# New places for the side pieces of an audio-tower kernel, and its softmax sums sent through 100 partitions for the reciprocal

## The reference, cut to what matters

```python
x.shape == (8, 120000)                       # 8 batches, 1500 frames of 80 samples
h = gelu(layernorm(frames @ W.T + b) * gamma + beta)          # tokenizer, 1500 x 256
n = layernorm(h)
Q, K, V = n @ Wq.T + bq, n @ Wk.T + bk, n @ Wv.T + bv         # 16 heads of 16
attn = softmax(Q K^T / 4)                                     # 1500 x 1500 per head
h = h + (attn @ V) @ Wo.T + bo
out = layernorm(h + ffn(layernorm(h)))
```

## Time and profile before

| | us |
|---|---|
| median of 3 runs | 2575.2 (2572.72 to 2577.77) |
| the profiled execution | 2566.03 |
| its span, first to last instruction | 2564.3 |
| PE busy | 2270.0 (89%) |
| ACT busy | 2154.9 (84%) |
| DVE busy | 1222.3 (48%) |
| POOL busy | 374.1 (15%) |
| DMA queues of SP, share of 16 engines | 19.1% |

### The profile page before, as it was taken

How to read it: one execution, slowest core, us unless ns; L and a number is a source line. 1 busy time by engine, 2 the same in 40 slices (tenths; PEclk the granted TensorE clock), 3 DMA queues, 4 the chain that set the end, 5 groups by cost and what they waited for, 6 DMA issues and landing times.

```text
span 2564.3 us, 48095 instructions
## 1 busy us (share of the span) xinstructions
PE 2270.0 (89%) x19500; PEld 680.2 (27%) x19500; DVE 1222.3 (48%) x2362; ACT 2154.9 (84%) x2332; POOL 374.1 (15%) x495
## 2 busy tenths in 40 slices
PE   4589998999989998899988999899998999898892
PEld 1222222222322222222222222222222222222221
DVE  6444435544465444643456444654446444452224
ACT  0099997999969998899978999699997999799991
POOL 2211002211121111210122110211112111120002
PEclk7799999999989999999989999899998999999997
DMA  2402211222122122122112221212212212111101
GB/s 60 128 17 63 63 37 39 53 63 63 38 69 56 42 59 53 46 77 53 41 45 53 63 63 39 58 40 56 67 33 70 54 51 53 52 47 31 31 5 30
DMA packets 89956, 132.09 MB, mean 52 GB/s; under 512 B 12295, under 2 KB 69702, under 8 KB 89726
## 3 DMA queue, kind: packets, MB, share of 16 engines
q1 hardware_dynamic: 87190, 127.11, 19.1%
...
## 4 chain that ended last, share of the span: by engine, by line
PE 40%; issue 34%; ACT 9%; POOL 9%; DVE 4%; POOLq 1%; DMA 1%; SPq 1%; DVEq 0%; ACTq 0%
PE PS L834 19%; PE PS L810 12%; PE PS L771 5%; ACT prob L476 4%; ACT prob L473 3%; POOL sq L367 3%; POOL Y L375 2%; PE PS L780 2%; POOL rs L377 2%; DVE HL L553 1%; POOL rs L348 1%; DVE HL L551 1%; POOLq L376 1%; DMA qk_halves_scratch<-HL 1%; ACT prob L481 1%
## 5 line engine op out<-in xcount | busy, mean ns | idle before, releaser
L834 PE MATMUL PS<-prob,Vst 125*32 125x500 f32 x9216 | 1149.8, 602 | 1.9 <-ACT prob L476 1.1
L481 ACT ACTIVATE prob<-PS 125x1000 f32<-125x1000 f32 x768 | 775.0, 1009 | 208.9 <-PE PS L810 208.3
L810 PE MATMUL PS<-QA,KA 64*125 64x500 f16 x4608 | 783.1, 413 | 105.2 <-DMA KA<-qk_halves_scratch 46.0
L473 ACT ACTIVATE prob<-PS 125x1000 f32<-125x1000 f32 x768 | 773.6, 1007 | 108.3 <-PE PS L810 108.2
L476 ACT ACTIVATE prob<-PS 125x1000 f32<-125x1000 f32 x768 | 782.8, 1019 | 0.0
L810 PEld LDWEIGHTS PS<-QA,KA 64*125 64x125 f16 x4608 | 258.7, 133 | 896.1 <-ACT prob L473 419.2
L603 DVE RECIPROCAL On<-Den 128x125 f32<-128x125 f32 x384 | 344.5, 918 | 10.2 <-issue 2.7
L834 PEld LDWEIGHTS PS<-prob,Vst 125*32 125x32 f32 x9216 | 221.9, 109 | 441.4 <-issue 272.9
L551 DVE TENSOR_SCALAR HL<-PS,b_qk 128x500 f16<-128x500 f32 x96 | 70.9, 738 | 397.9 <-PE PS L771 333.8
L367 POOL TENSOR_TENSOR sq<-HL 128x2000 bf16<-128x2000 f16 x24 | 84.5, 3522 | 1184.8 <-DVE HL L553 1184.8
L771 PE MATMUL PS<-zT,w_qk 128*32 128x500 f32 x1536 | 196.4, 593 | 1.2 <-DVE zT L542 1.2
...
## 6 DMA issues: line engine op xcount, KB each, us to landing
qk_halves_scratch<-HL SPq DMA_DIRECT2D x384, 125.0 KB
QA<-qk_halves_scratch SPq DMA_DIRECT2D x64, 375.0 KB, 5.0
KA<-qk_halves_scratch SPq DMA_DIRECT2D x64, 375.0 KB, 7.2
oT<-On SPq DMA_DIRECT2D x384, 31.2 KB, 2.0
...
```

The lines of the kernel that those rows point to most:

```text
L473: act.activation(prob[0:T, 6 * p:6 * p + 2, :], PS[0:T, 0:2, 0:QC], ACT.Exp, scale=scl)\
L481: act.activation(prob[0:T, 6 * p + 4:6 * p + 6, :], PS[0:T, 4:6, 0:QC], ACT.Exp, scale=scl)\
L810: last = pe.matmul(PS[0:T, bank, 0:QC], KA[rows, G % 2, h // 2, t * T:(t + 1) * T], QA[rows, G % 2, h // 2, c * QC:(c + 1) * QC], start=Tr ...
L834: last = pe.matmul(PS[lo:lo + 2 * HD, 6 + n % 2, 0:QC], Vst[:, b % 2, t, g * HG + j, :], prob[0:T, (HG * t + j) % 12, :], start=(t == 0), ...
```

## The change

Four things change together.

1. The plan. Places of nearly all pieces move, NORMS and GELU too. `tok` 0 and 1 of a batch now run in units 10 and 11 of the batch two before.
2. Reciprocals. `take_sums` no longer shuffles; it only copies. SP sends the 4 rows of sums (4 x 500 values) from `Osb` to a tile `thin` of 100 partitions by 20 values at the head of the unit after (`spread_sums`), DVE takes the reciprocal of `thin` in round 3 (`invert`), SP sends it back to rows 0, 32, 64 and 96 of `Den` in round 3 (`gather_sums`), and in round 5 DVE shuffles each of these rows over its 32 partitions and multiplies with `Osb` (`normalise`).
3. SP's order. `store_attended` moves to round 5, all `load_group` to the end of the list of the second unit of the group before (unit 10 for the next batch's first group), `store_out` of the third chunk to unit 3.
4. `tok_norm` subtracts the mean (and frees the bank) before it waits for POOL's root.

```diff
-    for j, r in enumerate((0, 2, 3, 4)):
+    for j, r in enumerate((0, 2, 4, 6)):
         place(11, r, "out", j)
         place(0, r, "out", 4 + j)
-    for j in range(2):
-        place(11, 5 + j, "tok", j)
-        place(0, 5 + j, "tok", 2 + j)
-        place(1, 2 * j, "tok", 4 + j)
-    place(1, 4, "out", 8)
+    place(10, 4, "tok", 0)
+    place(11, 3, "tok", 1)
+    place(0, 3, "tok", 2)
     for j in range(3):
-        place(1, 6, "out", 9 + j)
-    place(2, 4, "turn", 0)
-    place(2, 6, "turn", 1)
-    place_qk(0, 3, 0, 2)
-    place_qk(1, 3, 3, 4)
+        place(1, 2 * j, "tok", 3 + j)
+        place(2, 1, "out", 9 + j)
+    place(1, 6, "out", 8)
+    place(2, 6, "turn", 0)
+    place(3, 0, "turn", 1)
+    place_qk(0, 3, 2, 3)
+    place_qk(1, 3, 4, 5)
     place(3, 6, "val", 0)
     place_qk(2, 4, 0, 2)
     place_qk(3, 4, 3, 4)
-    place(4, 6, "val", 1)
-    place(5, 0, "val", 2)
+    place(4, 5, "val", 1)
+    place(4, 6, "val", 2)
+    place(5, 0, "val", 3)
     place(5, 1, "norm", 0)
-    place(5, 2, "val", 3)
-    place(5, 3, "turn", 2)
-    place(5, 4, "turn", 3)
-    place(5, 6, "val", 4)
-    place_qk(4, 6, 0, 2)
-    place_qk(5, 6, 3, 4)
+    place(5, 2, "turn", 2)
+    place(5, 3, "turn", 3)
+    place_qk(4, 5, 4, 6)
+    place_qk(5, 6, 0, 2)
+    place_qk(6, 6, 3, 4)
+    place(6, 5, "val", 4)
     place(6, 6, "val", 5)
-    place_qk(6, 7, 0, 2)
-    place_qk(7, 7, 3, 4)
-    place(7, 6, "val", 6)
-    place(8, 0, "val", 7)
+    place_qk(7, 7, 0, 2)
+    place(7, 3, "val", 6)
+    place(7, 4, "val", 7)
+    place(7, 6, "turn", 4)
+    place(8, 0, "turn", 5)
     place(8, 1, "norm", 1)
-    place(8, 2, "turn", 4)
-    place(8, 3, "turn", 5)
-    place_qk(8, 8, 4, 6)
-    place_qk(9, 9, 0, 2)
-    place_qk(10, 9, 3, 4)
-    place(9, 6, "val", 8)
-    place_qk(11, 10, 0, 2)
-    place(10, 3, "val", 9)
-    place(10, 4, "val", 10)
-    place(10, 6, "val", 11)
-    place(11, 1, "norm", 2)
-    place(11, 5, "flag", 0)
-    NORMS = {(2, 0): 0, (4, 6): 1, (7, 6): 2}
-    GELU = (1, 7)
+    place_qk(8, 8, 2, 3)
+    place_qk(9, 8, 4, 5)
+    place(8, 6, "val", 8)
+    place_qk(10, 9, 0, 2)
+    place_qk(11, 9, 3, 4)
+    place(9, 6, "val", 9)
+    place(10, 0, "val", 10)
+    place(10, 1, "norm", 2)
+    place(10, 2, "val", 11)
+    place(10, 6, "flag", 0)
+    NORMS = {(2, 3): 0, (4, 4): 1, (6, 6): 2}
+    GELU = (2, 2)
...
+            def spread_sums(n):
+                sp.wait_ge(s_ov, at(s_ov, n + 1))
+                sp.dma_start(thin[:, :], Osb[HD:128:2 * HD, :].rearrange("j (s c) -> j s c", s=25)).then_inc(s_pk, 16)
+
+            def gather_sums(n):
+                sp.wait_ge(s_rc, at(s_rc, n + 1))
+                sp.dma_start(Den[0:128:2 * HD, :].rearrange("j (s c) -> j s c", s=25), thin[:, :]).then_inc(s_up, 16)
...
-                    if u % NC == 1 and u < NU - 2:
-                        load_group(b * NG + u // NC + 1)
-                    if u < 3 and b > 0:
-                        store_out(b - 1, u)
+                    if n > 0:
+                        spread_sums(n - 1)
+                    if u in (0, 1, 3) and b > 0:
+                        store_out(b - 1, min(u, 2))
...
-                        if r == 4 and n > 0:
+                        if r == 3 and n > 0:
+                            gather_sums(n - 1)
+                        if r == 5 and n > 0:
                             store_attended(n - 1)
-                    if u == NU - 1 and b + 1 < B:
-                        load_group((b + 1) * NG)
+                    if u % NC == 1 and n + 2 < B * NU:
+                        load_group(n // NC + 1)
...
             def tok_norm(b, i, bank):
                 p, e = i % 2, hslot(b, 2 * i)
-                dve.wait_ge(s_r1, at(s_r1, b * (NT // 2) + i + 1))
+                dve.drain()
...
                 ins.then_inc(s_free, 1)
                 dve.drain()
+                dve.wait_ge(s_r1, at(s_r1, b * (NT // 2) + i + 1))
...
-                dve.stream_shuffle(Den[:, :], PS[:, 6 + n % 2, 0:QC], [HD + i % HD for i in range(2 * HD)])
                 dve.tensor_copy(Osb[:, :], PS[:, 6 + n % 2, 0:QC]).then_inc(s_ov, 1)
 
-            def invert(n, part):
-                if part == 0:
-                    dve.drain()
-                    if n > 0:
-                        dve.wait_ge(s_os, at(s_os, 64 * n))
-                dve.reciprocal(On[:, part * T:(part + 1) * T], Den[:, part * T:(part + 1) * T])
-                if part == CT - 1:
-                    dve.drain()
-                    dve.tensor_tensor(On[:, :], On[:, :], Osb[:, :], ALU.mult).then_inc(s_on, 1)
+            def invert(n):
+                dve.wait_ge(s_pk, at(s_pk, 16 * (n + 1)))
+                dve.reciprocal(thin[:, :], thin[:, :]).then_inc(s_rc, 1)
+
+            def normalise(n):
+                dve.wait_ge(s_up, at(s_up, 16 * (n + 1)))
+                dve.stream_shuffle(Den[:, :], Den[:, :], [0] * (2 * HD))
+                dve.drain()
+                if n > 0:
+                    dve.wait_ge(s_os, at(s_os, 64 * n))
+                dve.tensor_tensor(On[:, :], Den[:, :], Osb[:, :], ALU.mult).then_inc(s_on, 1)
...
-                    if 1 <= r <= CT and n > 0:
-                        invert(n - 1, r - 1)
+                    if r == 3 and n > 0:
+                        invert(n - 1)
+                    if r == 5 and n > 0:
+                        normalise(n - 1)
```

More of the change, by code:

```diff
@@ L94, in batch_of @@
         if what == "tok":
-            return b + 2 if u == NU - 1 else b + 1
+            return b + 2 if u >= NU - 2 else b + 1
         return b + 1
@@ L166, in audio_tower @@
         Den = sb("Den", [128, QC])
+        thin = sb("thin", [HG * 25, QC // 25])
         On = sb("On", [128, QC])
@@ L201, in audio_tower @@
             "s_wsq", "s_top", "s_root", "s_scl", "s_sq", "s_nm", "s_nm1", "s_rerun", "s_flag"))
-        s_sc, s_ex, s_pv, s_ov, s_on, s_os = (sem(n) for n in (
-            "s_sc", "s_ex", "s_pv", "s_ov", "s_on", "s_os"))
+        s_sc, s_ex, s_pv, s_ov, s_pk, s_rc, s_up, s_on, s_os = (sem(n) for n in (
+            "s_sc", "s_ex", "s_pv", "s_ov", "s_pk", "s_rc", "s_up", "s_on", "s_os"))
         s_ms, s_mx, s_wsum = sem("s_ms"), sem("s_mx"), sem("s_wsum")
@@ L219, in audio_tower @@
             s_nm1: B, s_flag: B, s_sc: 3 * PER * per_unit, s_ex: 3 * PER * per_unit, s_pv: NT * per_unit,
-            s_ov: per_unit, s_on: per_unit, s_os: 64 * per_unit,
+            s_ov: per_unit, s_pk: 16 * per_unit, s_rc: per_unit, s_up: 16 * per_unit, s_on: per_unit, s_os: 64 * per_unit,
             s_s1: per_tile, s_r3: per_tile, s_y: per_tile, s_yst[0]: 8 * per_chunk, s_yst[1]: 8 * per_chunk,
@@ L293, in run @@
                                 store_halves(pb, i)
-                        if r == 4 and n > 0:
+                        if r == 3 and n > 0:
+                            gather_sums(n - 1)
+                        if r == 5 and n > 0:
                             store_attended(n - 1)
-                    if u == NU - 1 and b + 1 < B:
-                        load_group((b + 1) * NG)
+                    if u % NC == 1 and n + 2 < B * NU:
+                        load_group(n // NC + 1)
+                spread_sums(B * NU - 1)
                 store_out(B - 1, 0)
+                gather_sums(B * NU - 1)
                 store_attended(B * NU - 1)
@@ L497, in _ @@
             dve.memset(Vst[:, :, :, :, :], 1.0)
+            dve.memset(Den[:, :], 1.0)
             def tok_stats(b, i, bank):
@@ L729, in run @@
                     finish_out(B - 1, e)
-                for part in range(CT):
-                    invert(B * NU - 1, part)
+                invert(B * NU - 1)
+                normalise(B * NU - 1)
                 for e in range(8, NT):
```

## The result

| | before | after |
|---|---|---|
| median of 4 runs, us | 2575.28 (2572.72 to 2577.77) | 2457.26 (2454.43 to 2458.36) |
| ratio, 95% interval | | 0.954 (0.9524 to 0.9557) |
| the profiled execution | 2566.03 | 2458.36 |
| its span | 2564.3 | 2456.6 |
| granted TensorE clock, mean over the span | 0.952 | 0.971 |

A forecast was written before the change was run, and what follows sets the result against it. ACT's floor bounds the kernel, with 34.5 us a batch of ACT waiting for PE to gain from. Prologue, batches (289.7 each for 1 to 5) and tail sum to 2464.9, 99.4 under the old span: median 2476, range 2446 to 2515.

The forecast's parts named there:

- likeliest case: Whole kernel: the main forecast of 2476 us, own range 2460 to 2495, chance 0.59.
- rival 1: Unit 4 does not stall as forecast: 2442 if all of it goes, 2458 for half; chance 0.17.
- (c): Unit 11: PE stands 11.89 in batch 6 for the late-issued group load; the largest item, gone after the change.
- Rival 3: Group load in unit 10 still ends late behind store_attended, most of (c) stays: +77, 2553; chance 0.03.
- (b): Single bank: unit 5's first piece stands 1.86 for s_ov; two tok in rounds that touch cost 2.80.
- rival 2: The clock falls in more places, at stalls in units 0, 7, 11 and the 0.5 pairs: 2505 to 2515; chance 0.17.
- (d): Clock: some 1.5 us at 1.2 GHz after unit 5's 1.86 stall, in some batches only.
- rival 4: Slower: gather lands over 10 us after issue in every unit, DVE stands at normalise; 2666 at 12 us; chance 0.04.
- the range of 0 to 1 us: Spread and gather transfers: bounds on their added cost per unit, forecast at 0.
- Even 7.2 is 1.7 late: Gather in units 3 and 8, behind four stores: even a 7.2 us landing costs PE 0.

The follow-up runs named there:

- e5: Changed kernel with the next batch's first group load back at the end of SP's list of unit 11; 2545.0 us, ratio 0.9901.
- e1: Kernel before with only the load of the next batch's first group moved from unit 11 to unit 10; 2524.66 us, ratio 0.9821.
- e10: e6 with every tok in an even round, plus a pending finish_out moved behind the next take_sums; 2400.53 us, ratio 0.933.
- e9: Changed kernel with the old tok_norm order, DVE waiting for POOL's root ahead of the first pass; 2473.16 us, ratio 0.9612.
- e8: Changed kernel with one more transfer, through a second buffer, on the reciprocals' way back to Den; 2473.45 us, ratio 0.9615.
- e6: Changed kernel with NORMS moved from (4, 4) and (6, 6) to (4, 0) and (6, 0); 2417.62 us, ratio 0.9404.
- e4: Changed kernel without the transfers: four reciprocals in rounds 1 to 4, shuffle in take_sums, product in round 4; 2492.65 us, ratio 0.9699.

## Why the prediction was right, and where it was off

**Sign and size.** Forecast 2476, measured 2457.3, within the range (2446 to 2515) and below the likeliest case's own range (2460 to 2495) by 2.7. Of the 18.7 between them, 8.3 are terms of the span (2464.9 forecast, 2456.6 measured) and the rest is the step from span to median. The 2457.3 also falls on what rival 1 gave for half of its case, 2458. By the time alone one would have believed that rival, and it is wrong: the stall that it doubts is there, 3.0 of 3.4.

**The sum is better than its terms: luck.** A batch was forecast at 289.7, and batches 1 to 5 take 288.6 on average. But units 3, 4, 8 and 11 were put too long, by 0.8, 0.8, 0.7 and 0.4, and units 1 and 5 too short, by 0.6 and 0.8, and the two kinds of error partly cancel. Each of them is taken up below.

**From span to median: the largest single miss.** I carried over that the median lay 9.2 above the profiled execution. After, that distance is -1.1. The runs of the kernel before, beside this result and beside the experiments, spread over 2565.4 to 2578.0, and the profiled one was a quick one among them; the changed kernel's runs spread over 3.9. So the 9.2 told where one execution had fallen in its spread, and nothing in the change carries it over. Without it the forecast would have been 2466.6.

**(c) the group load: right.** Unit 11 was forecast at 23.8 and is 23.4. e5 shows that this place is worth 88 us or a little more in the changed kernel, and e1 that it is worth 44.5 in the old one, where the `tok` chain is next. Rival 3 is out: no PE wait for `KA` is left in the loop.

**(b) the waits of 1.0 behind a `tok` and of 0.5 behind a `qk`: one term wrong, the time at which PE wants the bank.** Units 3 and 8 were forecast at 24.6 and 24.7 and are 23.8 and 24.0, near the 23.6 of unit 6, which has two odd pieces and no such pair. The end of DVE's work was forecast well, PE's need was not. In unit 3 of the changed kernel, and then the row of the kernel before that follows the last one of the earlier trace rows:

```profile
1068.72 1.02 PE L790 MATMUL PS<-zT,w_qk 128*32 128x500 f32 x8
...
1070.69 0.74 DVE L568 SCALAR_TENSOR_TENSOR HL<-PS,b_qk,HL 128x500 f16<-128x500 f32 x1
...
1071.48 1.05 PE L790 MATMUL PS<-zT,w_qk 128*32 128x500 f32 x8
```

```profile
517.14 1.02 PE L771 MATMUL PS<-zT,w_qk 128*32 128x500 f32 x8
```

DVE ends its second pass at 1071.43, 1.69 after PE's end at 1069.74 (1.65 forecast), and PE goes on 1.74 after it. Undisturbed, the next piece's matmuls start at 517.14, 1.57 after the end at 515.57. I had taken the weight load's start, 516.73, and so 1.16. The wait that is left is 0.17, and ACT has that in hand, for it starts its next exponentials on time. The 0.8 and 0.7 a batch are 10.5 over seven batches, more than the whole 8.3. The same term makes the stall behind an odd `tok` 2.1 - 1.57 = 0.5 instead of 1.0; PE's row says 0.4, and unit 11 is 23.4 against 23.8. Unit 0 is 23.8 as forecast, but that is luck: there the smaller stall behind the `tok` is made up by a wait for the Osb copy that I did not have, 0.45 by e10 (below). In the prologue 5.7 was forecast for `tok_norm`; it is 122.77 - 117.08 = 5.7, and e9 gives back 5.8; with the scatter of this stretch (e8) both are good to about 1.

**Unit 4: right to 0.1 us in the chain, 0.8 off in the sum.** From PE's end at 1095.97 the squares end at 5.3 (5.3 forecast), the root at 6.7 (6.8), `z` at 8.1 (8.2), `val` at 8.4 (8.7); PE wanted the bank at 5.5 (5.4). The stall is 2.98 against 3.3 to 3.4. The unit is 27.7 against 28.5, but unit 5 is 23.6 against 22.8, since the slow clock goes on into it (22.95 to 24.26 by batch, and 22.76 in e6, where it does not fall). e6 shows the whole of it in one edit. Rival 1 had the stall away for reasons that the trace does not bear out.

**The clock (rival 2): no.** The stalls of 1.1 in unit 7, 0.4 in units 0 and 11 and 0.3 in round 1 left the granted clock at 1.00. The stall of 2.98 brought it down in six of its seven batches (0.92 in unit 4 and 0.95 in unit 5 of batch 3) and not in batch 0. The only other fall in the loop is in unit 2 of batch 0 (0.88), where PE has no `out` to do under the gelu and waits 4.7 for ACT. The 6.29 us at 0.54 are what (d) had at 1.5, and they cost more: 1.2 in unit 4 (27.77 - 21.9 - 1.7 - 2.98) and on average 0.8 in unit 5, some 2 together, as the comparison with batch 0 has it too.

**Units 0 and 1: a term I did not have.** Unit 1 was forecast at the floor, 21.9, and is 22.5. Now that an `out` stands in round 6 of units 11 and 0, its `finish_out` is in DVE's list ahead of the next `take_sums`, and the Osb copy comes late for PE:

```profile
1010.23 1.07 PE L774 MATMUL PS<-w_tok,X 81*32 81x256 f32 x16 [0.26 <-DVE Osb L611]
```

e10 takes `finish_out` away from there, and both units fall to 22.0.

**The transfers (rival 4 and the range of 0 to 1 us): right in the result, with less room than I wrote.** The quiet landing is 1.9, from the issue to the end of DVE's wait, where I had 2 to 3:

```profile
1123.51 0.61 SPq L268 DMA_DIRECT2D Den<-thin  x1
...
1125.42 0.01 DVE L619 LOAD_MASK_SELECT Den<-Den  x1 [1.94 <-DMA Den<-thin]
```

"Even 7.2 is 1.7 late, and the next PE wait is a round or more away: 0" was true for units 3 and 8, to which it was applied, and not for unit 0, where `invert` runs late behind the `tok` of round 3 (1000.70, 17.8 into the unit) and the gather with it. There 2.7 more costs 0.9 to 1.3 a unit (e8). I had reckoned from SP's list alone and not from DVE's order in the round. In e5 the same oversight was the size of the miss. The Trainium skill (DMA: Bandwidth & Descriptors, Anatomy of one DMA) gives every transfer a fixed part of about 2.0 us beside its bytes, for GpSimd's path; the 1.9 here, on SP's, agrees. The warning on runs below 512 B, which the prediction took from the same page of the Trainium skill, shows no price here: packets below 512 B went from 12295 to 32263, the quiet landing is no longer than the 2.0 of `oT`, and no PE wait names these transfers.

**The reciprocals: under-sold.** I counted only the shuffle for them. e4 puts the new way of making them at 35 to 41. About half of that is unit 4, where `val` is taken 2.4 later in e4; and by the rows of e4 the cause there is the place of the product, beside POOL's squares in round 4, and not the reciprocals' own time. In the plan as changed, then, moving the product to round 5 keeps a bad place from being worse; whether the transfers would bring as much beside e6's NORMS was not tried. The one reciprocal that is left takes 0.27, where 0.15 to 0.2 was forecast.

**Prologue, batch 0, batches 1 to 6, batch 7, tail.** 117.08 (117.1 forecast), 288.6 (291), 1729.2 (1736.3), 268.0 (266.9), 53.7 (53.6).
